# Second feed-forward through the four chosen experts only: rows sorted into expert regions by scatters, expert weights addressed by a register

## What is computed

```python
    x = x + jnp.tanh(g_xattn[1]) * _L1_xattn_ref(_layernorm(x), ctx_1024, mask_1x1xSxS2_bk0, ...)
    x = x + jnp.tanh(g_ffn[1]) * _L1_ffn_ref(_layernorm(x), gate_w, e_bias, gate_proj, up_proj, down_proj, ...)

def _gate(x_flat, gate_w, e_bias):                     # N_EXPERTS 16, N_GROUP 4, TOPK_GROUP 2, TOP_K 4
    scores = jax.nn.sigmoid(x_flat @ gate_w.T)
    scores_for_choice = scores + e_bias[None, :]
    top2, _ = jax.lax.top_k(scores_for_choice.reshape(T, N_GROUP, 4), 2)
    _, group_idx = jax.lax.top_k(top2.sum(-1), TOPK_GROUP)
    ...                                                # score 0 outside the two chosen groups
    _, topk_idx = jax.lax.top_k(tmp_scores, TOP_K)
    topk_weight = jnp.take_along_axis(scores, topk_idx, axis=1)
    topk_weight = topk_weight / (topk_weight.sum(-1, keepdims=True) + 1e-20) * 2.5
    return topk_idx, topk_weight

    inter = jax.nn.silu(x @ gate_proj.T) * (x @ up_proj.T)     # for each of the 16 experts
    y = sum over the four chosen experts of topk_weight * (inter @ down_proj.T)
    out = y + (silu(x @ shared_gate_w.T) * (x @ shared_up_w.T)) @ shared_down_w.T
```

## Time and profile before

| | us |
|---|---|
| three runs | 1694.09, 1694.59, 1696.14; median 1694.59 |
| profiled execution, its own time | 1697.74 |
| its span in the trace | 1696.0 |
| `attend`, from 406 to 1046.6 in the trace | 640.6 |
| `gated_first` and `gated`, from 1046.6 to the end | 649.4 |
| busy PE, DVE, ACT, POOL | 1449.4, 1036.1, 761.3, 389.1 |

### The profile page before, as it was taken

The page is one execution under the profiler, slowest core; times in us unless marked ns, Lnnn a source line. Parts: engine busy times, 40 slices in busy tenths (PEclk is TensorE's granted clock), DMA queues, the critical chain, the costliest instruction groups (busy, mean ns, idle before and its releaser), DMA issues. The chain is left out here.

```text
span 1696.0 us, 27221 instructions
## 1 busy us (share of the span) xinstructions
PE 1449.4 (85%) x10184; PEld 1289.7 (76%) x10184; DVE 1036.1 (61%) x2075; ACT 761.3 (45%) x1927; POOL 389.1 (23%) x281
## 2 busy tenths in 40 slices
PE   3775229995899999999999986867999999999998
PEld 2554128894788888888888876756888888888887
DVE  4886855551765666666666664588555555555555
ACT  4554125552566566556666564521333333333332
POOL 4342263532000000000000001422333333333332
PEclk8666559997999999999999997979999999999999
DMA  3432834545000000000000000000000000000002
GB/s 95 134 105 74 184 114 123 138 123 134 7 8 7 14 7 8 8 8 8 8 7 8 2 1 20 1 20 10 10 10 19 9 9 10 18 9 9 9 0 99
DMA packets 55033, 67.18 MB, mean 40 GB/s; under 512 B 4096, under 2 KB 49312, under 8 KB 54944
## 3 DMA queue, kind: packets, MB, share of 16 engines
q1 hardware_dynamic: 37168, 47.92, 9.5%
q10 hardware_dynamic: 13808, 12.80, 2.3%
q0 software_dynamic: 3968, 5.25, 1.9%
HBM read 48.40 MB, written 17.56 MB: 39 GB/s over the span
## 5 line engine op out<-in xcount | busy, mean ns | idle before, releaser
L1883 DVE SCALAR_TENSOR_TENSOR const_acc<-gated_psY,const_weight,const_acc 128x256 f32<-128x256 f32 x512 | 212.5, 478 | 97.0 <-PE gated_psY L83 96.9
L1836 POOL TENSOR_TENSOR gheld_il<-gheld_it,gheld_ih 128x512 fp32r<-128x512 f32 x128 | 165.1, 1290 | 363.9 <-ACT gheld_ih L1858 363.9
L1193 ACT ACTIVATE attend_s<-attend_s,attend_less 128x128 f32<-128x128 f32 x512 | 198.8, 393 | 104.2 <-DVE attend_less L1307 104.2
L1858 ACT ACTIVATE gheld_ih<-gheld_it 128x512 fp32r<-128x512 f32 x128 | 80.8, 631 | 215.6 <-DVE gheld_it L1890 215.6
L1890 DVE TENSOR_TENSOR gheld_it<-gheld_sg,gated_psU 128x512 f32<-128x512 f32 x128 | 88.0, 687 | 135.8 <-PE gated_psU L83 128.9
L81 PE MATMUL gated_psY<-gheld_wh,gheld_il 128*128 128x256 f32 x512 | 145.4, 284 | 11.8 <-POOL gheld_il L1836 11.8
L1856 ACT ACTIVATE gheld_sg<-gated_psG 128x512 f32<-128x512 f32 x128 | 76.5, 597 | 164.9 <-PE gated_psG L83 152.0
L1650 POOL IOTA gheld_rank<- 128x16 f32 x1 | 0.1, 149 | 647.0 <-POOLq L1062 647.0
L83 PE MATMUL gated_psY<-gheld_wh,gheld_ih 128*128 128x256 f32 x512 | 145.6, 284 | 0.0
L82 PE MATMUL gated_psY<-gheld_wl,gheld_ih 128*128 128x256 f32 x512 | 145.6, 284 | 0.0
L1305 DVE SCALAR_TENSOR_TENSOR attend_s<-attend_psS,held_bias 128x1024 f32<-128x1024 f32 x64 | 78.0, 1219 | 62.6 <-PE attend_psS L1425 62.6
(11 more groups left out here) (321 smaller groups left out, 4134.0 us busy)
## 6 DMA issues: line engine op xcount, KB each, us to landing
layer_raw<-in_wi_dram SPq DMA_DIRECT2D x8, 1024.0 KB, 4.9
layer_raw<-in_wo_dram SPq DMA_DIRECT2D x8, 1024.0 KB, 6.9
gheld_raw<-in_gex_dram SPq DMA_DIRECT2D x17, 384.0 KB, 3.0
mix_xin<-in_x_dram SPq DMA_DIRECT2D x8, 512.0 KB, 4.4
mix_cin<-in_ctx_dram SPq DMA_DIRECT2D x8, 512.0 KB, 5.4
x_rows<-mix_x ACTq DMA_DIRECT2D x8, 512.0 KB, 2.9
xn_rows<-mix_xn ACTq DMA_DIRECT2D x8, 512.0 KB, 2.9
attend_cin<-in_ctx_dram SPq DMA_DIRECT2D x16, 256.0 KB, 2.7
```

What stands on the lines that cost most here:

```text
L1193: last = nc.scalar.activation(s[:, g, j, :], s[:, g, j, :], ACT.Exp, bias=less[:, g, j:j + 1], accum_out=sm[:, g, j:j + 1])
L1836: nc.gpsimd.tensor_tensor(G.il[:, j % 2], G.it[:, j % 2], G.ih[:, j % 2], ALU.subtract).then_inc(i_lo, 1)
L1858: nc.scalar.activation(G.ih[:, j % 2], G.it[:, j % 2], ACT.Copy).then_inc(i_hi, 1)
L1883: last = v.scalar_tensor_tensor(a, psY[j % 2][:, i, :], C["weight1"][:, j * BLOCK + i, bass.ds(e, 1)], a, ALU.mult, ALU.add)
```

## The change

`gated_first` and `gated` are gone, and one stage, `moe`, takes their place. The router moves into `attend` for batches 0 to 23, and into the first part of `moe` for batches 24 to 31.

**In `attend`.** As soon as 8, 8, 4 and 4 batches are finished, POOL normalizes their rows, two batches at a time (`normed`), SP stores them in DRAM (`normed_rows`), PE turns them and makes logits (12 pairs of batches), ACT exponentiates, and DVE picks groups and experts, makes weights, counts with PE's help how many rows before each chose the same expert, and turns the counts into four target rows for each row. This work on DVE stands in four parts for each chunk behind the batches named in the table of the diff. SP loads each batch of rows back, with its weights behind the numbers of a row (288 numbers), and POOL sends each batch out four times by an indirect DMA, a row to each of its four experts' regions (`slots`). There are 24 x 4 such sends for the first 24 batches, the last 16 of them in `moe`, and 8 x 4 for the last 8 batches, in `moe`.

**In `moe`.** All 17 experts' weights are kept split in SBUF. Work goes in pairs of subtiles, 2 x 128 rows. 16 pairs are the shared expert over all rows, and in these the 17 experts' weights are loaded and split, one in each pair (ACT high, DVE low, 1536 columns each). Then come 56 pairs for the regions of batches 0 to 23 and 24 pairs for those of batches 24 to 31: the number is fixed for the fullest case, 80 pairs. Which expert a subtile belongs to stands in a table that DVE makes from the counts. PE reads the place of the weights from it into a register (`base_of`, two reads for a pair), SP the place of the rows and of their weight (four reads for a pair, and four transfers: two of 128 rows x 1 KB, two of 128 x 8 bytes). In a pair PE turns the rows (4 transposes), makes gate and up (12 matmuls of 256 columns, now with the rows stationary), turns the inner values (2 transposes) and makes down (6 matmuls of 256). ACT splits and weighs, DVE splits and multiplies, and POOL scatters the weighted answers to DRAM (`answers`, two indirect DMAs for a pair). The unused ends of the regions are overwritten by `pads` so that they point to spare rows. Last, for each two batches, the four answers of each row are loaded (1 MB) and added on DVE (`combine`, 16 of them, 12 during the last 24 pairs and 4 at the end).

The router's part stands between a batch's statistics and the low parts for a coming step. The core of the diff:

```diff
+CHUNKS = ((0, 8), (8, 8), (16, 4), (20, 4), (24, 8))
+INSIDE = 4
+PART_OF = (0, 0, 0, 0, 1)
+PART_START, PART_B = (0, 24), (24, 8)
+REGION = tuple((n + 1) * P for n in PART_B)
+WIDE = D + 2 * E1
+MOST = 8
...
+    def store_normed(self, sp, c, i):
+        k = self.pairs_before(c) + i
+        b = CHUNKS[c][0] + 2 * i
+        sp.wait_ge(self.ln_up, k + 1)
...
+    def load_row(self, sp, c, t):
+        k = self.batches_before(c) + t
+        r, before = k % 2, k // 2
+        b = CHUNKS[c][0] + t
+        sp.wait_ge(self.idx_up, c + 1)
+        sp.wait_ge(self.xh_in, 16 * (self.pairs_before(c) + t // 2 + 1))
+        if before:
+            sp.wait_ge(self.sent[r], 16 * TOP * before)
+        sp.dma_start(self.row[:, r, 0:D], self.XH[b * P:(b + 1) * P, :]).then_inc(self.row_in[r], 16)
+        sp.dma_start(self.row[:, r, D:WIDE], self.meta[:, c % 2, t, :]).then_inc(self.row_in[r], 16)
+    def send(self, pool, c, t, ks=range(TOP)):
+        k = self.batches_before(c) + t
+        r = k % 2
+        pool.wait_ge(self.row_in[r], 32 * (k // 2 + 1))
+        pool.wait_ge(self.idx_up, c + 1)
+        for a in ks:
+            self.nc.gpsimd.indirect_dma_start(out=self.XS[PART_OF[c]], out_offset=bass.IndirectOffsetOnAxis(ap=self.idx[:, c % 2, t, a:a + 1], axis=0),
+                                              in_=self.row[:, r, :], in_offset=None).then_inc(self.sent[r], 16)
...
+    def choose_groups(self, dve, c):
...
+    def choose_experts(self, dve, c):
...
+    def weigh(self, dve, c, gate):
...
+    def place(self, dve, c, counts, free):
...
+    def index(self, dve, c):
...
+        self.groups = first({13: 0, 21: 1, 25: 2, 28: 3})
+        self.experts = first({14: 0, 22: 1, 26: 2, 29: 3})
+        self.weights = first({15: 0, 23: 1, 27: 2, 30: 3})
+        self.counted = first({16: 0, 24: 1, 28: 2, 31: 3})
+        self.rows = {17: [(0, 0), (0, 1)], 18: [(0, 2), (0, 3)], 19: [(0, 4), (0, 5)], 20: [(0, 6), (0, 7)],
+                     25: [(1, 0), (1, 1)], 26: [(1, 2), (1, 3)], 27: [(1, 4), (1, 5)], 28: [(1, 6), (1, 7)],
+                     29: [(2, 0), (2, 1)], 30: [(2, 2), (2, 3)]}.get(at, [])
...
+            R.make_consts(pool)
+            for i in range(4):
+                normed(0, i)
+            normed(1, 0)
+            send(0, 0, 1)
...
+    NX, NY, NR = 4, 3, 2
...
+            def load(j):
+                b = j % NX
+                if j >= NX:
+                    sp.wait_ge(t_done, j - NX + 1)
+                q = part_of(j)
+                if q is None:
+                    if 2 * j >= CHUNKS[LAST][0]:
+                        sp.wait_ge(R.xh_in, 16 * (R.pairs_before(LAST) + (2 * j - CHUNKS[LAST][0]) // 2 + 1))
+                    sp.dma_start(xg[:, b], R.XH[2 * j * P:2 * (j + 1) * P, :].rearrange("(a p) d -> p a d", p=P)).then_inc(x_in[b], 16)
+                    return
+                if j - NX >= SHARED_PAIRS:
+                    sp.wait_ge(y_up, j - NX + 1)
+                    sp.wait_ge(d_up, j - NX - SHARED_PAIRS + 1)
+                for s in range(2):
+                    at = (j - STARTS_OF[q]) * 2 + s
+                    block_ = sp.value_load(table[0:1, q, 1, at:at + 1], min_val=0, max_val=E1 * REGION[q] // P + E1 - 1)
+                    e2 = sp.value_load(table[0:1, q, 2, at:at + 1], min_val=0, max_val=2 * E1 - 2)
+                    r = bass.ds(block_ * P, P)
+                    sp.dma_start(xg[:, b, s, :], R.XS[q][r, 0:D]).then_inc(x_in[b], 16)
+                    sp.dma_start(wd[:, b, s, :], R.XS[q][r, bass.ds(e2 + D, 2)]).then_inc(x_in[b], 16)
...
+            def pads(q):
+                sp.wait_ge(table_up, 2 * q + 2)
+                sp.wait_ge(made, 4)
+                for e in range(E1):
+                    row = sp.value_load(tail[0:1, q, e:e + 1], min_val=0, max_val=E1 * REGION[q])
+                    sp.dma_start(R.XS[q][bass.ds(row, P), :], pad[:, q, :]).then_inc(pad_in, 16)
+                spare = R.XS[q][E1 * REGION[q]:E1 * REGION[q] + E1 * P, :].rearrange("(t p) n -> p t n", p=P)
...
+                if j == 10:
+                    pads(0)
+                if j == STARTS_OF[0]:
+                    ready(0, LAST)
+                at = j - sends_from - 2
+                if at >= 0 and at % TOP == 0 and at // TOP < CHUNKS[LAST][1]:
+                    R.load_row(sp, LAST, at // TOP)
...
+                if j == STARTS_OF[1] - 12:
+                    pads(1)
+                if j == STARTS_OF[1]:
+                    ready(1, LAST + 1)
+                load(j)
+                if j == STARTS_OF[1] + 7:
+                    answered(0)
+                if j >= STARTS_OF[1] + 7 and asked < COMBINES[0] and (asked < 2 or j >= STARTS_OF[1] + 7 + asked * 8 // 5):
+                    answers(asked)
+                    asked += 1
...
+            def scatter(j):
+                q = part_of(j)
+                pool.wait_ge(d_up, j - SHARED_PAIRS + 1)
+                pool.wait_ge(y_up, j + 1)
+                for s in range(2):
+                    nc.gpsimd.indirect_dma_start(out=R.YT[q], out_offset=bass.IndirectOffsetOnAxis(ap=dst[:, j % NX, s:s + 1], axis=0),
+                                                 in_=yb[:, j % NY, s, :], in_offset=None).then_inc(y_free[j % NY], 16)
...
+            for j in range(SHARED_PAIRS, PAIRS_ALL):
+                scatter(j)
+                at = j - sends_from
+                if 0 <= at < TOP * CHUNKS[LAST][1]:
+                    R.send(pool, LAST, at // TOP, (at % TOP,))
...
+            def y_out(j):
+                act.wait_ge(y_done, j + 1)
+                if j >= NY:
+                    y_read(act, j - NY)
+                if part_of(j) is None:
+                    nc.scalar.activation(rows(yb[:, j % NY]), psY[j % 2][:], ACT.Copy, scale=C["gate"][:, 3:4]).then_inc(y_up, 1)
+                    return
+                act.wait_ge(x_in[j % NX], x_count(j))
+                for s in range(2):
+                    last = nc.scalar.activation(yb[:, j % NY, s, :], psY[j % 2][:, s * D:(s + 1) * D], ACT.Copy, scale=wd[:, j % NX, s, 0:1])
+                last.then_inc(y_up, 1)
...
+            def combine(k):
+                q = int(k >= COMBINES[0])
+                dve.wait_ge(yt_in[k % 2], 16 * (k // 2 + 1))
+                a, y = acc[:, k * CB:(k + 1) * CB, :], yt[:, k % 2]
+                v.tensor_tensor(y[:, :, 0:2 * D], y[:, :, 0:2 * D], y[:, :, 2 * D:4 * D], ALU.add).then_inc(c_step, 1)
+                dve.wait_ge(c_step, 2 * k + 1)
+                v.tensor_tensor(y[:, :, 0:D], y[:, :, 0:D], y[:, :, D:2 * D], ALU.add).then_inc(c_step, 1)
+                dve.wait_ge(c_step, 2 * k + 2)
+                if k == 0:
+                    y_read(dve, SHARED_PAIRS - 1)
+                v.tensor_tensor(a, a, y[:, :, 0:D], ALU.add).then_inc(c_up, 1)
...
+            def base_of(j, s):
+                q = part_of(j)
+                if q is None:
+                    return 0
+                at = (j - STARTS_OF[q]) * 2 + s
+                return pe.value_load(table[0:1, q, 0, at:at + 1], min_val=0, max_val=E1 * PER)
...
+            def up(j, bases):
+                pe.wait_ge(x_lo, j + 1)
                 if j >= 2:
                     pe.wait_ge(i_up, j - 1)
-                G.up(pe, SHARED, slice(j * N, (j + 1) * N), psG[j % 2], psU[j % 2], g_done, u_done)
-                if j + 1 < BLOCKS:
-                    logits(j + 1)
+                for s in range(2):
+                    for k in range(KD):
+                        r = slice(k * N + s * P, k * N + (s + 1) * P)
+                        last = product(pe, psU[j % 2][:, s * 2 * I1:(s + 1) * 2 * I1], (xh[:, j % 2, r], xl[:, j % 2, r]),
+                                       [part(w, bases[s], k * 2 * I1, 2 * I1) for w in (wh, wl)], k == 0, k == KD - 1)
+                last.then_inc(u_done, 1)
...
+                former, bases = bases, [base_of(j, s) for s in range(2)]
+                if j:
+                    turn_inner(j - 1)
+                up(j, bases)
+                if j:
+                    down(j - 1, former)
+                if j + 2 < PAIRS_ALL:
+                    turn(j + 2)
```

More of the change, by code:

```diff
@@ L1058, in attend @@
+TURNED = {9: (0, 0), 10: (0, 1), 11: (0, 2), 12: (0, 3), 17: (1, 0), 18: (1, 1), 19: (1, 2), 20: (1, 3),
+          21: (2, 0), 22: (2, 1), 25: (3, 0), 26: (3, 1)}
+AT = [HalfStep(at) for at in range(B)]
+def attend(nc, A, C, held, X2, acc, stat3, R):
     STEPS, NB = B // 2, 2
@@ L1168, in _, with routed @@
             load(1, 1, 0)
+            def routed(half):
+                if half.turned:
+                    R.store_normed(sp, *half.turned)
+                for c, t in half.rows:
+                    R.load_row(sp, c, t)
             def body(n, p, h):
@@ new lines, in _ @@
+            last.then_inc(made, 1)
+            add(0)
+            R.send(pool, LAST - 1, 2)
+            add(1)
+            R.send(pool, LAST - 1, 3)
+            for j in range(2, SHARED_PAIRS):
+                add(j)
```

(14 more changed lines are left out.)

1082 lines of the change are left out of this document (685 added, 397 removed).

## The result

The change makes the kernel slower: 1806.56 us (four runs, 1804.58 to 1811.05) against 1694.34 for the kernel before, a ratio of 1.0664, 95% interval 1.0640 to 1.0687. The forecast was 1660 with a range of 1570 to 1765, so a gain of 35 us was expected and a loss of 112 came out. The profiled execution took 1804.76 with a span of 1803.0.

What follows compares the result with a forecast made beforehand. PE was taken to bound the old kernel, and the ring through SP to decide most of the new sum. `moe` at 582 against 649.4 us (-67) and attention +32 gave -35: 1660 us, range 1570 to 1765.

Steps and rivals of the forecast that it cites:

- start: Start of `moe`: first weights land, ACT and DVE split them, with issue and hops: 8 us.
- end: End of `moe`: last scatter's landing, four 1 MB loads, last sums, the store and its end: 26 us.
- The ring, 5.4 us a pair: Chain from `y_up` through SP, transfer, PE and ACT: 10.9 us for two pairs; 24 routed pairs priced at it, 130 us.
- The Trainium skill's figure: SP's and PE's register reads: about 600 ns a tensor load would make a pair 6.05 us; 0.4 was taken.
- 32 pairs under POOL, 5.7 us: First 32 routed pairs in `moe`: POOL's scatters plus a send set the pace, 5.7 us a pair, 182 us.
- Pads, +9 and +12: SP's queue in `moe`: pad reads and issues ahead of the loads cost +9 in the shared pairs, 12 later.
- Shared pairs, 4.3 us: First 16 pairs of `moe`: ACT 3.6 and DVE 3.3 us, with waits 4.3 each, 69 us; 78 with pads.
- Combines, +0.7 us a pair: Last 24 pairs: 12 combines' 1 MB loads in SP's queue, 1.4 us of each counted; 6.1 a pair, 146 us.
- Attention, +32: Routing work in `attend`: PE +13, DVE +10, POOL's lateness +9; sum +32 us.
- rival 1: SP's and PE's register reads make the ring slower: 6.6 us a pair, 1755 us; chances 0.22, plus 0.10 for about 0.6 us.
- Rival 2: In `moe` the ring is hidden and POOL alone decides: 496 us for the stage, time 1575; chance 0.20.
- Rival 3: The attention pays because DVE's work there isn't covered: +70 instead of +32, time 1698; chance 0.13.

Runs made afterwards that it cites:

- exp. 4: Changed kernel with the 18 pad transfers of each part spread over SP's stream instead of in one block: 1774.81 us, ratio 1.0474.
- exp. 9: Changed kernel with 8-deep row-weight slots, spread pads, one read a subtile, and ACT rounding the next expert's weights ahead of `moe_yb`: 1563.79 us, ratio 0.9234.
- exp. 12: Kernel of exp. 9 with combines one pair later and the second set of pads read and issued by ACT: 1548.1 us, ratio 0.9134.
- exp. 1: Changed kernel with the slots of the row weights and scatter addresses 8 deep instead of 4: 1667.28 us, ratio 0.9823.
- exp. 2: Changed kernel with SP reading each of a subtile's two numbers twice: 1890.9 us, ratio 1.1141.
- exp. 7: Changed kernel, slots still 4 deep, with SP reading one packed number a subtile instead of two: 1767.95 us, ratio 1.0460.
- exp. 10: Changed kernel with each combine of part 0 one pair later on DVE, its loads unmoved: 1784.76 us, ratio 1.0527.
- experiment 5: Changed kernel with 14 unused matmuls of 512 columns on PE in the wait of every second pair: 1781.43 us, ratio 1.0497.
- experiment 3: Kernel of exp. 1 (8-deep slots) with SP reading each of a subtile's two numbers twice: 1825.1 us, ratio 1.0768.
- experiment 11: Changed kernel with PE's routing work in the attention (transposes and gate product) done twice: 1820.43 us, ratio 1.0730.
- experiments 3 and 6: The second of these: changed kernel with 8-deep row-weight slots and spread pads together: 1643.3 us, ratio 0.9709. The first has its own line under experiment 3.
- 1573 us: Changed kernel with 8-deep row-weight slots, spread pads and one read a subtile together: 1573.36 us, ratio 0.9283.

## Why the prediction was wrong

The mechanism was named rightly: a ring of two pairs from `y_up` through SP, the transfer, PE and ACT. Its size was not, and other terms beside it were too small. By the prediction's own steps, `moe` in us, forecast and trace:

| step | forecast | trace | cause, and what shows it |
|---|---|---|---|
| start | 8 | 10.6 | |
| 16 shared pairs, first pads | 78 | 120.0 | pads 21 of it (exp. 4), order on ACT and DVE, and its meeting with POOL, 12 to 15 (exp. 9, 12); the other 84 to 87, against 69, stay open |
| 56 pairs of part 0, second pads | 324 | 393.8 | ring 6.7 a pair (exp. 1, 2, 7), pads 18 (exp. 4) |
| 24 pairs with combines | 146 | 178.6 | DVE's wait for the answers, 22 to 28 of it (exp. 10) |
| end | 26 | 31.6 | |
| sum | 582 | 734.6 | |

The fourth row ends at the last pair but none, at 1771.4; its rest is in the end's. `moe` is 153 us above its forecast: 70 are the routed pairs of part 0 (64 the ring, 6 the pads), 42 the shared pairs, 33 the last pairs, 8 start and end. The attention came out 10 below its forecast.

- *The ring, 5.4 us a pair.* This is the step that failed: the term was mis-sized. Forecast 10.9 us for two pairs, trace 13.6. SP has 4.5 for four reads and three issues where I had 2.9. Some 1.0 of the difference is the reads: one costs 0.56 to 0.6 us, not 0.4, with its check and the gaps, and the load of 0.61 makes one longer. The other 0.6 is the issues, 0.53 to 0.59 each with their address operations instead of 0.42. PE's part, to its last write, is 6.1 instead of 4.9, because the matmuls behind the wait run at a granted clock of 0.50, 1.2 GHz, where I had taken 0.75 (experiment 5 gives back 0.75 us a pair). PE's own two reads are not in the difference: the gap where they stand is 0.75, and I had priced them at 0.8. The landing was right (2.1 against 2.0), and ACT (0.85 against 1.0).
- *The Trainium skill's figure.* The prediction quoted "DMA: Bandwidth & Descriptors", section "Latency and other measured facts": a floor of about 600 ns for a tensor load. The instruction alone took 0.27 us here (L2056 above), so the row does not agree with it as the price of the load; doubled reads cost 0.6 us each with all that belongs to one (experiment 3), and this does. I had the case as a rival with 0.32 and chose 0.4 for no better reason than nearness to 0.17.
- *32 pairs under POOL, 5.7 us.* Wrong in cause. POOL's instruction takes 0.97 us and its period is 1.27, so three are 3.8 us, under SP's 4.8 to 5.2. I took the spacing of 1.88 from scatters in `experts` where another 0.99 stood beside them; the fast one was the rule. The ring decided there too.
- *Pads, +9 and +12.* I priced 18 issues at 0.82 us; they are 1.06 us, and the loads stand at most four pairs ahead of both sets. Spreading them gave back 21 and 18 us (experiment 4).
- *Shared pairs, 4.3 us.* I summed each engine's work and added 0.7 for waits; the trace has 5.5. The ring of experiment 9 goes through ACT and DVE by the order of the code and can't be seen in sums; it is at most 1 us a pair, and why a shared pair takes 5.1 without it stays open. My working, and the section on the change, also took an expert's weights as 1536 columns and 786 KB; they are 768 and 384 KB (`moe_wl` above is 128x768), so the start and this term were too high in work and still too low in time.
- *Combines, +0.7 us a pair.* I charged SP for them, not DVE: the wait for 5.4 us of landing stands on DVE ahead of the next `il`. With the ring there each combine's wait is added to a pair's path.
- *Attention, +32.* Trace +21.8. PE's own work is most of it: +13 was forecast, and doubling it cost 11 to 14 us in the timed runs (experiment 11). Some 8 us are left for what I charged to DVE (+10); no run varies it. POOL is not late (+9 forecast): its sends come every 1.27 us, not 1.88, and PE never waits for `router_xn` in the trace's list of waits of the attention. The shared port of "SBUF — State Buffer", section "SBUF: two separate sides" in the Trainium skill (DVE and POOL share it and one holds it for a whole instruction; a DVE operation with two SBUF inputs does so only against a POOL instruction that reads SBUF) changed little for the sends: of 80 in the attention the median is 0.972 us and the longest 1.848. Beside the combines, where I had allowed up to 2.5 us more, the 47 scatters have a median of 0.968 and a longest of 1.912. Where the trace agrees with that section is in the shared pairs: DVE's `moe_wl` takes 1.41 us instead of 0.96 when POOL's addition has begun before it (experiment 9; waiting for the addition's end and then working 0.96 would make 1.55). I had not looked for it there.

```profile
L1162 POOL DMA_INDIRECT slots<-router_row,router_idx x80: 965/972/1848, 775.4 to 1029.8; - x80
```

(instruction, count, then the shortest, median and longest in ns). Of the rivals, rival 1 (a slower ring) was right in place and, at 6.8 us a pair, also near its size of 6.6; its 1755 lacked the shared pairs and the combines. Rival 2 (POOL alone, 1575) was wrong: with the ring away SP decides, not POOL (experiments 3 and 6). Even at 1573 us the pace is near that of SP's stream: 1.79 and 1.86 us a subtile at the least, so 3.7 a pair of 4.0. Rival 3 (the attention, +70) was wrong, at +21.8.

## What to carry to other kernels

When a DMA's slot is released only at the end of a work item, and the DMA's address must first be read on the issuing queue, price the whole turn (release, reads, landing, engine, last reader) and divide by the items that one turn advances. Here these are two pairs though the slots are four deep, since PE turns the rows of a pair two pairs ahead. Making the small slot deeper cost nothing here and gave 139 us. Then price the queue itself: 0.6 us a read, 0.34 an issue and 0.53 to 0.59 with its address operations, and put runs of them where the queue has slack. In-order engines make rings of their own; find them by asking, for each wait, what stands queued behind it.
